# A two-layer graph kernel in fp32 on one core: adjacency blocks transposed in place, products over four chunks, and rows dealt out in fours

## What is computed

```
h   = adj @ (adj.T @ e)
y   = layernorm(x + layernorm(h) * gamma + beta + x)
deg = adj.sum(axis=0) + 1;  dinv = 1 / sqrt(deg)
z   = dinv * (y @ W)
o   = relu(dinv * (adj.T @ z + z) + b)
out = layernorm(y + o)
```

## Time and profile before

| | us |
|---|---|
| runs | 641.88, 644.96, 643.8; median 643.8 |
| profiled execution | 644.01 |
| its span, first to last instruction | 642.3 |
| TensorE busy | 605.3 (94%) |
| DVE / ACT / POOL busy | 317.0 / 138.9 / 106.7 |
| moved | 204.10 MB, 318 GB/s in the mean |

### The profile page before, as it was taken

How to read it: one execution, slowest core, us unless ns; L and a number is a source line. 1 busy time by engine, 2 the same in 40 slices (tenths; PEclk the granted TensorE clock), 3 DMA queues, 4 the chain that set the end, 5 groups by cost and what they waited for, 6 DMA issues and landing times.

```text
span 642.3 us, 15855 instructions
## 1 busy us (share of the span) xinstructions
PE 605.3 (94%) x7310; PEld 292.2 (46%) x7310; DVE 317.0 (49%) x347; ACT 138.9 (22%) x208; POOL 106.7 (17%) x126
## 2 busy tenths in 40 slices
PE   6899999999999999999999998999999999978774
PEld 4435545554554555455554566554443434313112
DVE  2577877757576876747586673212040402203004
ACT  2003260603305060421506054111000101001001
POOL 3055250401305050220505031100000000000000
PEclk9999999999999999999999999899999999999998
DMA  8998869595977959596895807999999999999992
GB/s 231 374 368 320 310 225 366 183 367 184 380 272 280 358 178 367 188 362 241 282 364 178 295 3 274 391 403 392 402 410 413 409 413 409 411 412 410 413 398 79
DMA packets 93221, 204.10 MB, mean 318 GB/s; under 512 B 14780, under 2 KB 14820, under 8 KB 93156
## 3 DMA queue, kind: packets, MB, share of 16 engines
q1 hardware_dynamic: 87556, 201.72, 84.1%
q10 hardware_dynamic: 5600, 1.38, 1.0%
HBM read 201.78 MB, written 1.31 MB: 316 GB/s over the span
## 4 chain that ended last, share of the span: by engine, by line
PE 80%; DMA 13%; DVE 3%; SPq 2%; ACT 1%; issue 1%; ACTq 0%
PE psum L755 34%; PE psum L852 22%; PE psum L940 12%; DMA slot<-in_adj_dram 6%; PE psum L860 5%; DMA cut_last<-in_adj_dram 3%; DMA cut<-in_adj_dram 3%; PE psum L796 2%; DVE cut L597 1%; DMA X<-in_x_dram 1%; PE psum L960 1%; PE psum L809 1%; PE psum L922 1%; PE psum L910 1%; SPq L253 1%; SPq L256 1%
## 5 line engine op out<-in xcount | busy, mean ns | idle before, releaser
L597 DVE STREAM_TRANSPOSE cut<-slot 128x2048 f32<-128x2048 f32 x80 | 177.8, 2280 | 62.6 <-PE psum L852 62.3
L755 PE MATMUL psum<-slot,E 128*64 128x512 f32 x888 | 201.7, 596 | 1.2 <-DMA slot<-in_adj_dram 0.8
L852 PE MATMUL psum<-cut,T 32*64 32x256 f32 x5120 | 147.9, 377 | 1.4 <-DVE cut L597 1.2
L852 PEld LDWEIGHTS psum<-cut,T 32*64 32x64 f32 x5120 | 115.1, 131 | 47.5 <-issue 30.2
L372 POOL COPY turned<-cut_last 32x1024 f32<-32x1024 f32 x80 | 82.7, 1034 | 252.7 <-PE psum L860 241.5
L755 PEld LDWEIGHTS psum<-slot,E 128*64 128x64 f32 x888 | 60.9, 137 | 123.2 <-issue 115.5
L415 ACT ACTIVATE turned<-cut_last 32x1024 f32<-32x1024 f32 x80 | 84.4, 1055 | 17.0 <-DVE cut_last L597 10.2
L406 ACT ACTIVATE T<-T 32x256 f32<-32x256 f32 x60 | 24.8, 414 | 239.1 <-DVE T L575 237.9
L698 DVE TENSOR_TENSOR T<-psum,dinv 128x256 f32<-128x256 f32 x10 | 4.2, 425 | 144.6 <-PE psum L960 144.2
L940 PE MATMUL psum<-slot,E 128*64 128x512 f32 x272 | 64.6, 596 | 6.2 <-DMA slot<-in_adj_dram 6.2
L940 PE MATMUL psum<-cut,E 128*64 128x512 f32 x224 | 53.4, 597 | 4.0 <-DMA cut<-in_adj_dram 4.0
(11 more groups left out here) (111 smaller groups left out, 295.5 us busy)
## 6 DMA issues: line engine op xcount, KB each, us to landing
slot<-in_adj_dram SPq DMA_DIRECT2D x136, 1024.0 KB, 8.7
cut<-in_adj_dram SPq DMA_DIRECT2D x35, 1024.0 KB, 17.3
cut_last<-in_adj_dram SPq DMA_DIRECT2D x10, 1024.0 KB, 13.5
turned<-in_adj_dram SPq DMA_DIRECT2D x10, 1024.0 KB, 17.5
X<-in_x_dram SPq DMA_DIRECT2D x5, 256.0 KB, 8.7
out_dram<-T ACTq DMA_DIRECT2D x10, 128.0 KB, 9.9
T<-in_L_gnn_W_u_dram ACTq DMA_DIRECT2D x2, 16.0 KB, 2.9
T<-in_L_gnn_W_i_dram ACTq DMA_DIRECT2D x2, 16.0 KB, 3.1
```

Of the source, the lines that this page charges most:

```text
L597: v.transpose(to.rearrange("p c (j k r) -> p j k c r", j=JB, r=Q32), slot[c % NS][:, :, :].rearrange("p k (j c r) -> p j k c r", j=JB, r=Q ...
L755: return mm(acc[half[b % 2], :], E[:, b, :], view[:, b % CB, :], start=(b < 2), stop=(b >= NB - 2))
L852: last = mm(acc[half[h], a, u * 2 * P:(u + 1) * 2 * P], T[step % 2][rows_a, jb, (c - a) % 4, :], cut[u][rows_a, c, h, :, jb * P:(jb + 1) * P],
```

## The change

Rows are dealt out in fours: row 512 q + 4 p + k of adj, x and out lies in partition p, block 4 q + k. A partition's four rows of a chunk are adjacent in HBM. X, out and the diagonals are thus moved in runs of 1 KB or more.

The nine slots, `cut` and `cut_last` go; there are two sets of eight places (`slot[0]`, `slot[1]`, by even and odd step) and two places `last_slot` for chunks 8 and 9. A chunk is transposed in its own place, and so only after it has been summed. All eight of the set are transposed ahead of copy_tT, chunks 8 and 9 behind copy_t. A set is loaded again when the products of its step are done, last_slot when the moves are.

The products of h take 512 columns over four chunks (0, 2, 4, 6 or 1, 3, 5, 7) at once; there are two rounds a step, of 20 sums and two groups of 32 products. In step 0 the sums are ahead in each round, in steps 1 to 8 the products.

Nothing is kept for the second layer: all 20 half chunks of round 0 are loaded, in pairs of strips like the later rounds. X is loaded ahead of the chunks. The degrees are turned by 16 small matmuls (`turn_degrees`) in step 9. The residual work of POOL on X goes behind its moves of steps 0 to 4. Two of the four `h_last` groups of step 9 come ahead of sum_h(0), two behind turn_y(0).

```diff
-NS = 9
-UNITS = 2
-UQ = 4
-SPARE = NB // CB * RES - NS
-T_ROUNDS = 4
+NF = 8
+T_ROUNDS = 2
...
+PLACES = [(0, q) for q in range(8)] + [(0, 8), (1, 8)] + [(1, q) for q in range(8)] + [(0, 9), (1, 9)]
...
+    x_rows = x.rearrange("(q p k) f -> p q (k f)", p=P, k=CB)
+    out_rows = out.rearrange("(q p k) f -> p q (k f)", p=P, k=CB)
+    adj_rows = adj.rearrange("(q p k) j -> p q k j", p=P, k=CB)
...
+        slot = [sb(f"slot{i}", [P, NF, CB, JW]) for i in range(2)]
+        last_slot = sb("last_slot", [P, NQ - NF, CB, JW])
+        turned = sb("turned", [P, 4, NQ - NF, CB, JB, Q32])
...
+            return slot[step % 2][:, q] if q < NF else last_slot[:, q - NF]
+        def chunk_loaded(step, q):
+            return (slot_loaded[step % 2][q], step // 2 + 1) if q < NF else (last_loaded[q - NF], step + 1)
...
+            for g in range(1, NG):
+                load_x(g)
             for c in range(NJ * NQ):
-                if c >= NS:
-                    n = c - NS
-                    if n % NQ == NQ - 1:
-                        sp.wait_ge(t_done, n // NQ + 1)
-                    else:
-                        sp.wait_ge(chunk_summed, n // NQ * (NQ - 1) + n % NQ + 1)
-                    sp.wait_ge(chunk_cut, cuts_by(n))
-                load(slot[c % NS][:, :, :], slot_loaded[c % NS], c % NQ, (c // NQ + RES) % NJ)
-                if c + 2 < NG:
-                    load_x(c + 2)
-                if c == NS - 1:
+                step, q = c // NQ, c % NQ
+                if q < NF and step >= 2:
+                    sp.wait_ge(slots_used, step - 1)
+                elif q >= NF and step >= 1:
+                    sp.wait_ge(moved_act, step * len(ACT_MOVES))
+                    sp.wait_ge(moved_pool, step * len(POOL_MOVES))
+                load(chunk(step, q), chunk_loaded(step, q)[0], q, (step + RES) % NJ)
...
+            for m, (s, q) in enumerate(PLACES):
+                if q == NF:
                     sp.wait_ge(moved_act, NJ * len(ACT_MOVES))
                     sp.wait_ge(moved_pool, NJ * len(POOL_MOVES))
-                elif m in (2, 5):
-                    sp.wait_ge(h_done, 1 if m == 2 else 2)
-                load_spare(m)
+                elif q > NF:
+                    sp.wait_ge(h_done, 2)
+                elif s == 0:
+                    sp.wait_ge(slots_used, NJ - 1)
+                else:
+                    sp.wait_ge(h_done, 1)
+                load_pair(0, m)
             for k in range(1, NJ // RES):
                 for m in range(RES * NQ):
-                    s, q = m % RES, m // RES
-                    if k == 1 and m == LATE:
-                        sp.wait_ge(h_done, 3)
-                        load_spare(SPARE - 2)
-                        load_spare(SPARE - 1)
-                    if k == 1 and q == NQ - 1:
-                        sp.wait_ge(acc_done, s + 1)
-                    elif k == 1:
-                        sp.wait_ge(chunk_swept, m + 1)
-                    else:
-                        sp.wait_ge(chunk_swept, RES * (NQ - 1) + (k - 2) * RES * NQ + m + 1)
-                    view, landed, _ = resident(s, q)
+                    sp.wait_ge(chunk_swept, (k - 1) * RES * NQ + m + 1)
+                    view, landed, _ = place(m)
                     if (k, m) >= TAIL:
                         load(view, landed, *tail_part(m))
                     else:
-                        sp.dma_start(pair[m], adj_rows[:, m * WB:(m + 1) * WB, k * RES * JW:(k + 1) * RES * JW])\
-                          .then_inc(landed, 16)
+                        load_pair(k, m)
...
+                pool.wait_ge(chunk_cut, (step + 1) * NQ)
                 if step >= 1:
                     pool.wait_ge(turned_used, step)
                 for a, c in POOL_MOVES:
-                    nc.gpsimd.tensor_copy(turned[c * Q32:(c + 1) * Q32, a, :, :],
-                                          cut_last[a * Q32:(a + 1) * Q32, c, :, :]).then_inc(moved_pool, 1)
+                    nc.gpsimd.tensor_copy(turned[c * Q32:(c + 1) * Q32, a].rearrange("p h k j r -> p (h k j) r"),
+                                          last_blocks[a * Q32:(a + 1) * Q32, :, c, :]).then_inc(moved_pool, 1)
                     moves += 1
                     pool.wait_ge(moved_pool, moves)
+                if step < NG:
+                    g = step
+                    pool.wait_ge(e_ready, g + 1)
+                    Xg = X[:, g * GB:(g + 1) * GB, :]
+                    link(nc.gpsimd.tensor_scalar(Xg, Xg, 2.0, None, ALU.mult))
+                    nc.gpsimd.tensor_tensor(Xg, Xg, feat(beta_b), ALU.add).then_inc(residual_ready, 1)
+                    pool.wait_ge(residual_ready, g + 1)
...
+                nc.scalar.activation(turn[J % RES][:, :].rearrange("p (k j) -> p k j", k=CB),
+                                     bank[J % 4].rearrange("p (j k) -> p k j", k=CB), ACT.Copy).then_inc(oT_ready, 1)
...
             def cut_chunk(c):
                 step, q = c // NQ, c % NQ
-                dve.wait_ge(slot_loaded[c % NS], (c // NS + 1) * 16)
-                if q < UNITS * UQ:
-                    u = q // UQ
-                    if step >= 1 and q % UQ == 0:
-                        dve.wait_ge(unit_used, (step - 1) * UNITS + u + 1)
-                    to = cut[u][:, :, q % 2, q % UQ // 2, :]
+                if q < NQ - 1:
+                    dve.wait_ge(chunk_summed, step * (NQ - 1) + q + 1)
                 else:
-                    if step >= 1 and q == UNITS * UQ:
-                        dve.wait_ge(moved_act, step * len(ACT_MOVES))
-                        dve.wait_ge(moved_pool, step * len(POOL_MOVES))
-                    to = cut_last[:, :, q % 2, :]
-                v.transpose(to.rearrange("p c (j k r) -> p j k c r", j=JB, r=Q32),
-                            slot[c % NS][:, :, :].rearrange("p k (j c r) -> p j k c r", j=JB, r=Q32))\
-                 .then_inc(chunk_cut, 1)
+                    dve.wait_ge(t_done, step + 1)
+                parts = by_part(chunk(step, q))
+                v.transpose(parts, parts).then_inc(chunk_cut, 1)
             def sum_degrees():
-                dve.wait_ge(t_ready, 2 * NJ)
-                late = RES * JB
-                link(v.tensor_scalar(mask[:, late:NB], deg[:, 0:NB - late], 1.0, None, ALU.add))
-                link(v.tensor_scalar(mask[:, 0:late], deg[:, NB - late:NB], 1.0, None, ALU.add))
+                dve.wait_ge(deg_turned, 1)
...
+                for q in range(NF):
                     cut_chunk(step * NQ + q)
                 copy_tT(step)
                 copy_t(step, step % 2)
+                for q in range(NF, NQ):
+                    cut_chunk(step * NQ + q)
                 if step == NJ - 1:
                     sum_degrees()
-                for q in late_:
-                    cut_chunk(step * NQ + q)
-                if 1 <= step <= NG:
-                    centre_residual(step - 1)
-                if step == NG + 1:
+                if 2 <= step <= NG + 1:
+                    centre_residual(step - 2)
...
+            def turn_degrees():
+                pe.wait_ge(t_ready, 2 * NJ)
+                for jb in range(JB):
+                    for k in range(CB):
+                        last = mm(deg_turn[jb * Q32:(jb + 1) * Q32, k, :], ident[:, k::CB], deg[:, jb::JB],
+                                  start=True, stop=True)
+                last.then_inc(deg_turned, 1)
...
+            def h_group(step, jb):
                 for c in range(4):
+                    cols = slice(jb * P + c * Q32, jb * P + (c + 1) * Q32)
                     for a in range(4):
                         rows_a = slice(a * Q32, (a + 1) * Q32)
                         for h in range(2):
-                            last = mm(acc[half[h], a, u * 2 * P:(u + 1) * 2 * P], T[step % 2][rows_a, jb, (c - a) % 4, :],
-                                      cut[u][rows_a, c, h, :, jb * P:(jb + 1) * P],
+                            last = mm(acc[half[h], a, :], T[step % 2][rows_a, jb, (c - a) % 4, :],
+                                      slot[step % 2][rows_a, h:NF:2, :, cols],
                                       start=False, stop=False, skip_group_check=True)
                 return last
             def h_last(step, jb):
                 for h in range(2):
-                    last = mm(bank[4][half[h], :], T[step % 2][:, jb, 0, :], turned[:, :, h, jb * P:(jb + 1) * P],
+                    last = mm(bank[4][half[h], :], T[step % 2][:, jb, 0, :], turned[:, :, h, :, jb, :],
                               start=False, stop=False, skip_group_check=True)
...
+                each = JB // T_ROUNDS
                 for n in range(T_ROUNDS):
-                    u, jb = n * UNITS // T_ROUNDS, n * UNITS * JB // T_ROUNDS % JB
-                    if not final:
+                    if step == 0:
                         t_pairs(step + 1, n * HS // T_ROUNDS, (n + 1) * HS // T_ROUNDS)
                     if n == 0:
                         pe.wait_ge(t_ready, step * 2 + 2)
```

(38 more changed lines are left out.)

155 lines of the change are left out of this document (70 added, 85 removed).

## The result

The changed kernel takes 648.13 us (median of 13 runs, 646.26 to 649.13), the kernel before 643.78 (13 runs, 641.63 to 647.01). The ratio is 1.0059 with a 95% interval of 1.0043 to 1.0075: slower by some 0.6%. 648.0 had been predicted. The profiled execution took 649.13 us, with a span of 647.2, so it lies 1.0 above the median.

What follows compares the result with a forecast made beforehand. The second layer was taken to be as long as its transfers from 388.6 us on; +3.05 (later loads), +2.56 (one more chunk), -1.65 (fewer 2 KB runs) and +0.2 (gap) made +4.2 on 643.8: 648.0 us, range 640.5 to 653.5.

Steps and rivals of the forecast that it cites:

- Start: First strip, with X loaded early: turn_t(1) ends 2.6 us earlier, 1.6 at copy_tT and 1.0 in step 0.
- The risk of chunks 8 and 9: Strip 1: these two chunks land near 66 and 68.5 us, when they are wanted; 0 to 1 us lost.
- A strip: Each first-layer strip takes 37.1 us for 36.8, with products 0.45 shorter; +0.3 eight times, +2.4 us.
- The 1.4 us at 293: First layer: 1.4 us lost once around 293 us, left in the sum; its absence taken into the range.
- copy_tT and the transposes: Each strip from step 1: 0.86 us between sums and turn_t; three transposes done at 8.6, half ending at 8.8.
- Handover: Between the layers: SP issues the first load behind the moves at 391.65 us, 3.05 us later than before.
- Stream: Second-layer loads: 92 chunks, not 91, +2.56 us; 11 fewer in 2 KB runs, -1.65; a gap of 0.2.
- the rival of the 80 KB pitch: Second-layer loads: rows in fours lower reads from 410 to 387 GB/s, +13 us; at half of this 654; chance 0.1.
- no holes worth counting: Second layer of the kernel before: its loads run from 388.6 us to the last chunk without pauses that matter.
- Tail: After the last chunk: 17 us; strided copy costing 0 to 1 and store saving 0.3 taken as zero together.
- Rival (a): Whole kernel: products and start gain more and the result is faster, together 7.9 us less, 640.1; chance 0.15.
- Rival (c): First layer: DVE becomes the bound of a strip, +0.4 to 1 us a strip, 651 to 656; chance 0.08.

Runs made afterwards that it cites:

- filler: The changed kernel with 11 bf16 matmuls of zeros put between the last sums of step 0 and turn_t(0): 646.76 us, 1.0034 to the kernel before.
- pad: The changed kernel with seven 512-column fp32 matmuls (about 6 us) added in round 0 of the second layer, behind turn_y(4): 647.82 us, 1.0051 to the kernel before.
- first7: The changed kernel with copy_tT ahead of the eighth transpose of step 0: 646.69 us, 1.0024 to the kernel before.
- narrow: The changed kernel with the products of h over two chunks (256 columns) again, twice the matmuls: 678.44 us, 1.0521 to the kernel before.
- narrow4: The changed kernel with 256-column products and four rounds a strip instead of two: 666.01 us, 1.0343 to the kernel before.
- oldpitch: The changed kernel with adj alone read in the old row order, partitions 20 KB apart (another output): 647.69 us, 1.0067 to the kernel before.
- xfirst: The kernel before with all of X loaded ahead of the chunks, nothing else changed: 644.67 us, 0.9992 to the kernel before.
- keep: The changed kernel with strip 1 kept, its eight chunks turned back in place by DVE, 12 chunks loaded for round 0: 639.18 us, 0.9915 to the kernel before.
- split: The changed kernel with the first of four column blocks of h_last ahead of turn_t instead of behind it: 646.74 us, 1.0046 to the kernel before.

## Why the prediction was right, step by step

The time was right to 0.1 us and the mechanism held (the second layer is its stream of loads; the change starts that stream later and makes it a chunk longer), but two terms ahead of it were wrong and cancelled in part. The 0.1 us are luck: the profiled execution missed by 0.7 us of span (647.2 for 646.5), and lay 1.0 above its median where that of the kernel before lay 0.2 above.

- **Start: wrong by 3.0 us.** The step was "Together -2.6 us at the end of turn_t(1)"; it was +0.4 (80.71 after 80.26). The terms themselves were near: E done at 24.95 (25.3 was said), the eighth transpose ending at 42.5 (43.1), t ready at 40.4 (40.9). What failed was to let the wait of 2.8 us cost only itself. The clock took another 3.2: turn_t 0.8 and the sums 2.4. filler shows it. In other executions of the same work the clock took less (pad's turn_t(1) ends at 79.40). The risk of chunks 8 and 9 came as 0.24 us. And first7 shows that the other loads of strip 1 stood close behind as well.
- **A strip: 37.06 for 37.1 said, with a term wrongly named.** The products did fall from 14.56 to 14.10. It was called mostly the width of the pass. narrow shows 7.09 against 7.05 a run for width, 0.08 a strip; the other 0.38 are that two long runs have fewer changes of shape than four short ones (7.09 in narrow, twice 3.64 in narrow4), 0.19 for each change and not 0.13. Width does count, by the number of instructions: at 256 columns the longer runs cost 21 us in stops.
- **The 1.4 us at 293** was left in, and is gone. Eight strips and it: +0.6 instead of the +2.4 of the sum. turn_t(9) ended at 377.16, 1.26 later than said.
- **copy_tT and the transposes: right.** 0.77 to 0.80 us between sums and turn_t in each of eight strips; three transposes of 2.27 us in the second half of the sums, just covered, as said; a transposed chunk costs the same in place.
- **Handover: right.** 15.9 us from turn_t(9) to SP's load, 15.75 said. Moves out of 32-element runs cost ACT 1054 ns (1055) and POOL 1058 (1034): no surcharge but 0.2 us. turn_degrees was mis-sized: 1.38 us and not 3. h_done was not on the path, so it cost nothing.
- **Stream: right.** 237.3 us from first load to last chunk; by the terms of the sum it is 1.5 + 236.1 + 0.2. The gap did not come. Rates of 410 in the windows, as before; the rival of the 80 KB pitch is out in this kernel by oldpitch. The page "DMA: Bandwidth & Descriptors" of the Trainium skill, section Latency and other measured facts, lists losses for row pitches that are large powers of two, from 512 KiB up. 80 KB is none of these, and the 410 GB/s measured at either pitch do not speak against it. What read wrongly was "no holes worth counting": the kernel before has 360 GB/s from 445 to 450 us, and xfirst shows that TensorE's path through the norms bound it almost as closely. That did not touch the forecast, because the changed kernel's stream starts later.
- **Tail: right**, 16.8 for 17.1.
- **Rival (a)** had one part that came true, the 1.4 us at 293. Its 2 us at the start did not come in this kernel; first7 shows that they were there to be had (2.3 us at the start of the stream). The products fell by 0.46 a strip and not by 0.76, and the rate stayed at 410. By the Trainium skill's page "TensorEngine Tiling (Array Packing)", Instruction Overhead, with some 60 cycles for each matmul, an estimate for the 16 passes (64 matmuls in tiles side by side) fewer in a run is 0.4 us; narrow shows 0.04. **Rival (c)** did not come: the last of the three transposes ended at 263.97 and the sums at 264.11.

## What to carry to other kernels

When two layers have different bounds, find the instant at which the second one's stream starts, and weigh each edit by what it does to that instant and to the number of chunks behind it. A buffer scheme that saves waits in a stage that had none pays nothing; here it also threw away nine chunks that were already on the chip, and turning them back on DVE, which had time, was worth 9 us (keep against the changed kernel), more than any other edit tried here. Count a wait on TensorE at its length and then at what the clock takes after it, and ask what arrives next once the wait is gone. Where an engine stops with nothing in the profile to wait for, count its instructions from stop to stop.

## What the runs showed of the hardware

- A wait of 2.8 us on TensorE was followed by a granted clock of 0.50, for 6.8 us in the changed kernel and for 3.4 in pad and split with the same wait; after 2.3 us of waiting (oldpitch) it was 6.8 us. Behind waits of 1.3 and 1.7 us (keep, narrow), and with the wait filled with matmuls (filler), it stayed at 1.00.
- Long bursts of short matmuls (256 records of 256 columns, a weight load each, 7.1 us) stopped 12 times for 1.2 to 2.5 us in one execution, ten times of 12 while transfers were at 374 GB/s or more. The stops lie whole multiples of 256 instructions apart and end 1.2 to 1.5 us after a 16 KB packet of the instruction queue has landed. With 512 columns a record, no burst of the first layer stopped.
- A 32x32 transpose of a 128x2048 tile in place takes 2.27 to 2.30 us, as out of place; products whose moving operand is read in runs of 32 elements lose nothing (128 records in 3.64 us in narrow4 as in the kernel before).
